# Weighted sum of a convolution and attention kernel in groups of four tiles, the convolution behind the group of step 5

## What is computed

```python
x = x + _L0_conv_ref(_gn(x), L0_conv_weight)          # group norm, 3x3 convolution 64 -> 64
t = _to_tokens(x)                                     # 3136 tokens of 64 channels an image
t = t + _L1_attn_ref(_ln_t(t), Wq, bq, Wk, bk, Wv, bv)    # full attention, one head, softmax
t = t + _L1_ffn_ref(_ln_t(t), gate_w, gate_b, w1, w2, w3) # 16 experts, the best 2 of a token
x = _from_tokens(t, x)
```

## Time and profile before

| what | value |
|---|---|
| median of 3 runs | 2724.68 us (2722.92 to 2728.44) |
| the profiled execution, its own time | 2721.7 us |
| span of its trace | 2720.0 us |
| PE busy | 2506.6 us, 92% |
| DVE busy | 1832.1 us, 67% |
| ACT busy | 1317.0 us, 48% |
| POOL busy | 1016.9 us, 37% |
| mean granted TensorE clock | 0.964 of full |

### The profile page before, as it was taken

The page is one execution under the profiler, slowest core; times in us unless marked ns, Lnnn a source line. Parts: engine busy times, 40 slices in busy tenths (PEclk is TensorE's granted clock), DMA queues, the critical chain, the costliest instruction groups (busy, mean ns, idle before and its releaser), DMA issues.

```text
span 2720.0 us, 46270 instructions
## 1 busy us (share of the span) xinstructions
PE 2506.6 (92%) x13821; PEld 1604.3 (59%) x13821; DVE 1832.1 (67%) x5227; ACT 1317.0 (48%) x2986; POOL 1016.9 (37%) x1097
## 2 busy tenths in 40 slices
PE   5899999999999999999999999999999999997773
PEld 3455555566666666566666666566665656554662
DVE  5577677767676777677766777676867776674432
ACT  2344444455555555455545555455555555453542
POOL 2022005300343425342444324442344324465665
PEclk8899999999999999999999999999999999997866
DMA  2033101111112122121212122222121111122432
GB/s 75 26 90 77 45 22 48 49 34 39 53 49 66 52 54 59 55 58 49 62 52 62 48 57 64 58 53 53 54 55 52 43 49 51 54 55 62 121 94 53
DMA packets 226556, 152.95 MB, mean 56 GB/s; under 512 B 100240, under 2 KB 216720, under 8 KB 226320
## 3 DMA queue, kind: packets, MB, share of 16 engines
q1 hardware_dynamic: 190880, 98.26, 13.7%
q0 software_dynamic: 31456, 48.03, 6.8%
q10 hardware_dynamic: 3984, 3.70, 0.6%
HBM read 83.92 MB, written 65.27 MB: 55 GB/s over the span
## 4 chain that ended last, share of the span: by engine, by line
PE 62%; DVE 14%; issue 5%; DMA 2%; POOL 2%; ACT 1%; SPq 1%; POOLq 0%; DVEq 0%; ACTq 0%
PE ps_o L1480 16%; PE ps_s L1468 8%; PE ps_m L1440 7%; PE ps_s L1469 7%; DVE max_part L1118 4%; PE ps_x L1639 4%; PE ps_z L1653 3%; PE ps_z L1506 3%; PE ps_x L1646 2%; PE ps_z L1628 2%; DMA tc<-kept 1%; PE ps_y L1543 1%; PE ps_y L1559 1%; PE ps_s L1639 1%; POOL got L780 1%
## 5 line engine op out<-in xcount | busy, mean ns | idle before, releaser
L1118 DVE TENSOR_REDUCE max_part<-ps_m 128x1 f32<-128x448 f32 x1400 | 858.3, 621 | 517.1 <-PE ps_m L1440 497.1
L951 ACT ACTIVATE prob<-ps_s 128x448 f32<-128x448 f32 x1400 | 757.3, 543 | 526.6 <-PE ps_s L1469 502.8
L1480 PE MATMUL ps_o<-prob,v_s 128*64 128x448 f32 x2800 | 682.8, 561 | 0.0
L1468 PE MATMUL ps_s<-q_a,k_a 128*128 128x448 f32 x1400 | 592.7, 423 | 1.7 <-ACT q_a L943 0.7
L780 POOL DMA_INDIRECT got<-sorted_y,slot x448 | 427.3, 954 | 433.7 <-PE ps_s L1469 216.6
L759 POOL DMA_INDIRECT sorted_x<-xn,slot x448 | 428.8, 957 | 350.8 <-issue 154.7
L1440 PE MATMUL ps_m<-k_a,q_a 128*128 128x448 f32 (+3 forms) x1600 | 531.1, 359 | 27.1 <-DVE max_part L1118 21.2
L1469 PE MATMUL ps_s<-q_b,k_a 128*128 128x448 f32 x1400 | 511.4, 365 | 0.0
L1440 PEld LDWEIGHTS ps_m<-k_a,q_a 128*128 128x128 f32 (+1 forms) x1600 | 298.6, 188 | 92.2 <-DVE max_part L1118 61.2
L1468 PEld LDWEIGHTS ps_s<-q_a,k_a 128*128 128x128 f32 x1400 | 265.3, 189 | 142.4 <-ACT prob L951 107.3
L1480 PEld LDWEIGHTS ps_o<-prob,v_s 128*64 128x64 f32 x2800 | 153.2, 135 | 225.2 <-issue 161.7
(11 more groups left out here) (190 smaller groups left out, 3033.6 us busy)
## 6 DMA issues: line engine op xcount, KB each, us to landing
fx<-sorted_x SPq DMA_DIRECT2D x43, 384.0 KB
sorted_y<-fy SPq DMA_DIRECT2D x42, 320.0 KB, 2.9
xh<-in_x SPq DMA_DIRECT2D x96, 126.0 KB, 2.7
fx<-sorted_x SPq DMA_DIRECT2D x47, 256.0 KB
sorted_x<-fy POOLq DMA_DIRECT2D x28, 320.0 KB, 6.0
sorted_x<-xn,slot POOLq DMA_INDIRECT x448
got<-sorted_y,slot POOLq DMA_INDIRECT x448
x_now<-in_x SPq DMA_DIRECT2D x112, 56.0 KB, 2.3
```

The lines of the kernel that those rows point to most:

```text
L951: a.activation(prob[(at.n * KEY_TILES + i) % PROBS][:], ps_s[(at.n * KEY_TILES + i) % 2][:, 0:CHUNK], ACT.Exp).then_inc(s["p_ready"], 1)
L1118: v.tensor_reduce(max_part[n % 2][0:here.stop - here.start, j, kb:kb + 1], ps_m[(passes_before(n) + m) % 2][0:here.stop - here.start, 0:CH ...
L1468: t.matmul(ps_s[t_of % 2][:, 0:CHUNK], k_a[p][:, keys], high, start=True, stop=False)
L1480: t.matmul(ps_o[side:side + CHANNELS, 0:CHUNK], v_s[u % 2][:, i, :], prob[(n * KEY_TILES + i) % PROBS][:], start=(i < 2), stop=(i >= KEY_T ...
```

## The change

The weighted sum goes in groups of four tiles: tiles 0 to 3 in step 5, 4 to 7 in step 9, then in steps 13, 17 and 21; the last five stay in step 1. The convolution moves from step 1 to step 5, directly behind the group there, and with it `normed` from 0 to 4, `convolved` from 2 to 6 and `tokens` from 3 to 7. Queries go from step 7 to 8, the second transposes from 10 to 11, the gate from 11 to 12, logits from 12 to 13, `picked` from 15 to 16, `compared` and the exponential from 16 to 17, `gates` and `route_pick` from 17 to 18. The first transposes go from 16 to 17. Numbers and sizes of all computing instructions stay as they are.

```diff
+STEPS = [(4, "pre", "normed"), (4, "post", "attended"), (4, "post", "residual"), (6, "pre", "convolved"),
+         (6, "post", "norm2a"), (7, "post", "norm2b"), (7, "pre", "tokens"), (8, "post", "apply2"),
...
+CONV_AT = 5
+STEPS.sort(key=lambda step: step[0])
...
-ASK_AT = 7
+ASK_AT = 8
...
-                    if routes and i == 17:
+                    if routes and i == 18:
                         route_pick(b)
...
-            def weigh(n, u, first, many=2):
+            def weigh(n, u, first, many=GROUP):
...
-                    if i % 2 == 1 and 0 <= first < LAST_GROUP and at.attends:
+                    if i % GROUP == 1 and 0 <= first < LAST_GROUP and at.attends:
                         weigh(at.n, at.u, first)
                     if i == 1 and at.active("post"):
                         weigh(at.index("post"), at.batch("post"), LAST_GROUP)
+                    if i == CONV_AT and at.active("pre"):
+                        conv(at)
```

More of the change, by code:

```diff
@@ L114 @@
 LAST = LATE + 2 * CHUNKS - 1
-STEPS = [(0, "pre", "normed"), (1, "pre", "conv"), (2, "pre", "convolved"), (3, "pre", "tokens"),
-         (4, "post", "attended"), (4, "post", "residual"), (6, "post", "norm2a"), (7, "post", "norm2b"), (8, "post", "apply2"),
-         (9, "stats", "stats"), (10, "post", "turned2"), (10, "pre", "norm1a"), (11, "post", "gate"), (11, "pre", "norm1b"),
-         (12, "post", "logits"), (13, "stats", "mean"), (13, "stats", "deviation"), (14, "stats", "variance"), (14, "stats", "scale"),
-         (14, "pre", "apply1"), (15, "post", "picked"), (16, "pre", "turned"), (16, "post", "compared"), (16, "post", "gate_exp"),
-         (17, "post", "gates")]
+STEPS = [(4, "pre", "normed"), (4, "post", "attended"), (4, "post", "residual"), (6, "pre", "convolved"),
+         (6, "post", "norm2a"), (7, "post", "norm2b"), (7, "pre", "tokens"), (8, "post", "apply2"),
+         (9, "stats", "stats"), (10, "pre", "norm1a"), (11, "post", "turned2"), (12, "post", "gate"), (11, "pre", "norm1b"),
+         (13, "post", "logits"), (13, "stats", "mean"), (13, "stats", "deviation"), (14, "stats", "variance"), (14, "stats", "scale"),
+         (14, "pre", "apply1"), (16, "post", "picked"), (17, "pre", "turned"), (17, "post", "compared"), (17, "post", "gate_exp"),
+         (18, "post", "gates")]
+CONV_AT = 5
+STEPS.sort(key=lambda step: step[0])
 EXPERT_STEPS = sorted(
@@ L1655, in expert @@
                     last.then_inc(s["y_done"], 1)
-            events = {"conv": conv, "tokens": tokens, "turned": turned,
+            events = {"tokens": tokens, "turned": turned,
                       "attended": attended, "turned2": turned2, "gate": gate, "mean": mean,
```

## The result

The changed kernel takes **2793.04 us** (median of 4 runs, 2788.73 to 2806.8); the kernel before, on the same chip, 2723.80 us (2720.41 to 2728.44). The ratio is 1.0262, interval 1.0222 to 1.0301: slower by 2.6%, where the prediction said no change (2729 us, range 2692 to 2758). The profiled execution of after took 2790.79 us with a span of 2789.1 us.

What follows compares the result with a forecast made beforehand. PE, busy 92%, was taken as the bound with DVE near; the groups' -85 us were given back as waits, +4 us in sum on 2721.7 us, so 2729 us by the median, range 2692 to 2758.

Steps and rivals of the forecast that it cites:

- groups, with the order of f32 work: Weighted sum: five pairs out, five rounds in per body, fewer returns between f32 and f32r matmuls; -85 us.
- convolution, from step 1 to step 5: Convolution behind four tiles, not five: no free half of the array for its first rows; +3 us.
- combining in step 0, two-product bodies, clock: Without the convolution in step 1, PE waits for DVE and tc in step 2, and the clock can fall; +5, +27, +13 us.
- chain to the second transposes, steps 9 to 12: DVE's longer, later-starting chain to q_b makes PE wait at the second transposes; +37 us, bounds 15 and 55.
- tokens in step 7: Tokens' transposes keep the wait they had in step 3; no extra cost, 0.
- routing in step 19: In seven bodies with routing, route_pick in step 18 no longer has PE weighing on the way to route_total; +6 us.
- combining of step 18, step 21: In 19 bodies step 18's combining leaves DVE about 0.55 us behind the product, with no pair covering; +10 us.
- steps 13, 16 and 17 (first transposes): First transposes stand behind a group in step 17 and lose their waits for DVE; -12 us.
- part 5: Remaining effects: combining of step 18 +10 us, routing +6 us, first transposes -12 us; SP, POOL and ACT nothing.
- rival (b): DVE becomes the bound between groups, PE waiting in steps 10 to 12 and 14 to 16; 29 us more, 2758 us; chance 0.22.
- part 1: Groups of four in place of pairs: a pair costs 1.00 to 1.10 us, a further round 0.75; -85 us.

Runs made afterwards that it cites:

- a_groups_only: Kernel before with only the weighted sum in groups of four; convolution and all later steps stay where they were: 2714.37 us, ratio 0.9967.
- c_tc_early: Changed kernel with the load of tc for combining in step 0 issued one body earlier, ahead of the store of the experts' rows: 2742.63 us.
- e_before_tc: Kernel before with only the load of tc for combining in step 0 issued ahead of the store of the experts' rows: 2710.59 us.
- s_later_only: Kernel before with only the later steps for queries, second transposes, gate, logits, first transposes and routing; pairs and convolution in step 1 kept: 2724.64 us.
- t_apply13: h_groups_tc_qb_t17 with VectorE's apply1 in step 13 in place of 14: 2670.79 us.
- f_groups_tc_qb: Kernel before with groups of four, tc loaded earlier and q_b first in its VectorE step; first transposes stay in step 16: 2670.57 us.
- b_conv_only: Changed kernel with the weighted sum in pairs again; convolution in step 5 and the later steps kept: 2743.97 us, ratio 1.0074.
- d_qb_first: Changed kernel with VectorE's q_b put ahead of its other work of step 9 (statistics and the experts' gating): 2768.59 us.
- r_conv1_qb: Changed kernel with convolution, its sum and the tokens' transposes back in steps 1 to 3, and q_b ahead of VectorE's other work of step 9: 2736.47 us.
- w_groups_qb: Kernel before with groups of four and VectorE's q_b at the head of its step 8: 2682.64 us.
- g_after_tc_qb: Changed kernel with both tc loaded one body earlier and q_b ahead of VectorE's other work of step 9: 2708.15 us.
- p_conv4: h_groups_tc_qb_t17 with the convolution in step 4, its sum in step 5 and the tokens' transposes in step 6: 2668.61 us.
- h_groups_tc_qb_t17: Kernel before with groups of four, tc loaded earlier, q_b first in its VectorE step and first transposes in step 17: 2660.90 us, ratio 0.9767.
- q_after_conv1: Changed kernel with the convolution, its sum and the tokens' transposes back in steps 1, 2 and 3; groups and later steps kept: 2786.55 us.

## Why the prediction was wrong

The terms against the ledger of after (55 bodies), a round at 41.3 us and pairs as in a_groups_only:

| term | predicted | measured |
|---|---|---|
| groups, with the order of f32 work | -85 | -76 |
| convolution, from step 1 to step 5 | +3 | -3 |
| combining in step 0, two-product bodies, clock | +45 | +40 (53 by c_tc_early less 13 by e_before_tc, steps 2 to 4) |
| chain to the second transposes, steps 9 to 12 | +37 | +21 |
| tokens in step 7 | 0 | +29 |
| routing in step 19 | +6 | +11 |
| combining of step 18, step 21 | +10 | +22 |
| steps 13, 16 and 17 (first transposes) | -12 | +26 |
| sum | +4 | +70 |

The groups: pairs out -272, rounds in +206, and the queries 10.5 cheaper in steps 7 and 8 by s_later_only. Tokens are what is left in steps 2, 3, 4, 7 and 8: c_tc_early stands there 18.7 us above e_before_tc when the pair is put back in, and 10.5 of the queries are added. The price of the groups was nearly right: a round costs 0.75 us as predicted, and a pair gave 0.76 in step 11 and 1.01 to 1.09 elsewhere, where 1.00 to 1.10 was predicted.

**The step that failed** is in part 5 and in the words against rival (b), "by my count DVE has caught up by step 14". From step 13 on I had expected +4 us and measured 59. Part 5 took 12 us off for the first transposes' waits, as work that ends behind a group of four. Before had only 5.5 us of such waits. They ended, but `apply1`, the picks and the codes still stand in DVE's steps 14 to 16, light steps of PE of 0.7 to 1.3 us in a row, and the two-ahead rule of the maximum products hands the wait to the product of step 17 (17.4 us of waits in 21 bodies). To this come step 21 (12.2 in 21), where part 5 had the combining at half its size, and step 19 (8.4 in 8). Recorded waits from step 13 on rise by 33 us; the rest of the 55 us by which the term was short was not traced wait by wait. Rival (b) comes nearest to what happened: DVE holds PE between the groups, but in steps 16 to 21, where it was expected in steps 10 to 16, and with more than its 29 us; it had a chance of 0.22. t_apply13 and f_groups_tc_qb moved single pieces within these steps, and the wait passed to the next product or to `hid`. This speaks for the amount of DVE's work there as much as for its order, though no run made it less.

**A second step failed: the tokens.** The prediction gave them in step 7 the wait that they had in step 3 and nothing more, and in part 1 it took the full price of a pair for step 7 too. But that pair would have covered their wait. Taking it out gave 60 us in a_groups_only and 23.5 between b_conv_only and after; 24.8 of the 36.6 us that are missing are waits for `x_conv`, in 49 bodies, where step 3 had 14.8 in 35.

**Combining in step 0** was right in mechanism and place and nearly in size. c_tc_early took 50.4 us off the changed kernel, but the same edit took 15 off the kernel before, so the change added 35 to 40 us, against 45 for the row. Of this 27 were for the wait and 13 for nine falls of the clock; ten of the 14 bodies have one. The Trainium skill (TensorE: Matmul & The Clock Gate, HAM oscillation — how this bites in real kernels) tells of matmuls that start cold behind each wait for a load. The trace agrees only in part: in body 22 3.40 us at 0.50 follow a wait of 2.64 us, but they begin 1.1 us after PE has started again, and behind the 3.33 us of body 26 the clock stays at 1.00.

**The chain to the second transposes** was predicted in its members, 53.8 us of waits where the text said 30 to 50, and its cause was half wrong. Statistics and gating ahead of `q_b` are the cause (d_qb_first, r_conv1_qb, w_groups_qb). The idle DVE beside the long group and the convolution is not: with the convolution in step 1 the same steps cost 59 us, with it in step 5 they cost 20. I had its sign wrong; I read this as time that DVE gets for residual and norm, which no run shows by itself. The Trainium skill (Perfetto Trace Analysis, Optimization Strategy) advises to look at the gaps of the bounding engine for what blocks it, and to make that start sooner or end faster. Here starting sooner was enough: q_b and tc, 85 us, with no operation made shorter.

**What stays open.** The terms overlap, as g_after_tc_qb shows (10 us more than its parts). How much of each is the clock can't be told: after has 15 half-clock stretches of 64.8 us between 95 and 2510 us and before has 3 of 30.7, but no run removes the falls without the waits. Of the tokens' 29 us only the 10 by which the waits for `x_conv` grew can be read from rows; the row rests on differences of several runs and is the least certain. Groups with the convolution in step 5 but with the steps of before for queries and transposes were not run, so how much of the loss that pair of parts makes is open. That p_conv4 is slower than h at all is hardly clear of noise.

## What to carry to other kernels

Two edits that cost nothing alone can cost 2.1% together (groups and later steps): groups make the light steps lighter, later steps put a chain's end into them, and only the pair showed it, so price the parts together and not one by one. In the same way an edit that removes a loss says what it costs now, and not what the change added: run it in the kernel before too. Where one engine is busy 92% and a second 67%, the question isn't the second's total but what stands in its queue ahead of each result that the first waits for; putting that result first (`q_b`) and issuing its load ahead of a slow store (`tc`) gave 85 us. Work of one engine that is moved away from a place uncovers all that it had covered there, the loads, a second engine's copy and the sum behind it, and each is to be looked up before the move.

## What the runs showed of the hardware

The granted clock can fall behind short waits. In q_after_conv1 it was 0.50 for 3.40 us in body 1, behind two waits of 0.62 and 0.56 us in three light steps:

```profile
187.96 0.47 PE L1442 MATMUL ps_m<-k_a,q_a 128*128 128x448 f32 x1 [0.62 <-DVE max_part L1120]
...
188.98 0.57 PE L1554 MATMUL ps_y<-ident,xn 112*128 112x112 f32 x4 [0.56 <-DVE q_b L1112]
```

```profile
191.10:194.50 3.40, 3.40 (x11) 1.52 (x12) 2.41 (x10) 0.54 (x1) 2.46 (x3) 0.50 0.00 0
```

That kernel had 16 such stretches, 78.5 us in all between 95 and 2510 us, h_groups_tc_qb_t17 5 of 37.5, all of them in the last 110 us. A longer wait doesn't always bring a fall: ten of the 14 combining bodies of after have one, but behind the 3.33 us of body 26 the clock stayed at 1.00. The clock record of q_after_conv1 holds no level but 0.5 and 1.0.
